# Position attention in a two-layer block: the residual sum moves from VectorE to TensorE and ScalarE

## The reference, cut to what matters

```
hidden = layernorm(x)                                  # [S=8, B=512, H=256]
ln1    = layer_norm(hidden, ln1_weight, ln1_bias)
q,k,v  = split(ln1 @ qkv_weight.T)                     # 16 query heads, 4 key/value heads, 16 wide
attn   = softmax(causal(q . k / 4))                    # over the positions 0..s
ao     = attn . v
h1     = hidden + ao @ proj_weight.T                   # <- the residual sum of this case
ln2    = layer_norm(h1, ln2_weight, ln2_bias)
logits = ln2 @ router_weight                           # then top-2 experts; h1 is also added later
```

## Time and profile before

| | |
|---|---|
| median of 3 runs | 1718.29 us (1713.36 to 1721.59) |
| the profiled execution | 1712.79 us, of which 1711.0 us are the span from its first to its last instruction |
| mean granted TensorE clock | 0.972 of full speed |
| busy shares over the span | PE 93%, DVE 55%, POOL 42%, ACT 37% |

### The profile page before, as it was taken

How to read it: one execution, slowest core, us unless ns; L and a number is a source line. 1 busy time by engine, 2 the same in 40 slices (tenths; PEclk the granted TensorE clock), 3 DMA queues, 4 the chain that set the end, 5 groups by cost and what they waited for, 6 DMA issues and landing times. The chain is left out here.

```text
span 1711.0 us, 33848 instructions
## 1 busy us (share of the span) xinstructions
PE 1596.6 (93%) x11520; PEld 1337.6 (78%) x11520; DVE 934.3 (55%) x2469; ACT 629.0 (37%) x1879; POOL 721.0 (42%) x849
## 2 busy tenths in 40 slices
PE   8999889999999878777699999997999999999998
PEld 6777778887888646676588888885788888888887
DVE  6545536666666695986612222115665565565552
ACT  3333345555555464446411111111333333333331
POOL 3222233333343387973333332315545545445432
PEclk9999989999999999888699999999999999999999
DMA  7686600000000000001433333321000000000000
GB/s 197 128 163 109 111 28 14 14 14 14 13 13 2 17 1 1 25 25 44 141 121 97 110 104 97 99 56 44 29 23 28 21 25 28 18 28 28 19 11 13
DMA packets 92656, 88.58 MB, mean 52 GB/s; under 512 B 11840, under 2 KB 82432, under 8 KB 92160
## 3 DMA queue, kind: packets, MB, share of 16 engines
q1 hardware_dynamic: 73776, 56.63, 13.7%
q0 software_dynamic: 6912, 18.88, 4.2%
q10 hardware_dynamic: 11856, 11.66, 2.0%
HBM read 46.64 MB, written 23.20 MB: 41 GB/s over the span
## 5 line engine op out<-in xcount | busy, mean ns | idle before, releaser
L711 POOL TENSOR_TENSOR probs<-probs,rs 128x384 f32<-128x384 f32 x128 | 105.9, 827 | 212.5 <-DVE rs L886 211.6
L2031 PE MATMUL n_psS<-f_XT,wgu 128*128 128x128 f32 x1536 | 182.2, 275 | 0.9 <-ACT f_XT L2151 0.8
L2031 PEld LDWEIGHTS n_psS<-f_XT,wgu 128*128 128x128 f32 x1536 | 176.6, 192 | 1.7 <-ACT f_XT L2151 1.6
L845 ACT ACTIVATE probs<-psS,nm 128x192 f32<-128x192 f32 x256 | 105.5, 417 | 142.0 <-DVE nm L882 142.0
L1712 POOL DMA_INDIRECT XE<-token_rows,held x80 | 76.1, 951 | 187.7 <-PE e_psX L1731 170.6
L1806 DVE COPY YE<-e_psY 128x512 f32<-128x512 f32 x40 | 27.7, 692 | 224.5 <-PE e_psY L1754 224.5
L1744 PE MATMUL e_psH<-e_XT,w 128*128 128x256 f32 x640 | 145.8, 381 | 0.0
L1754 PE MATMUL e_psY<-w,e_HT 128*128 128x256 f32 x640 | 144.5, 379 | 0.0
L1754 PEld LDWEIGHTS e_psY<-w,e_HT 128*128 128x128 f32 x640 | 121.6, 190 | 16.5
L1782 ACT ACTIVATE e_HT<-e_psH 128x512 f32<-128x512 f32 x80 | 47.7, 597 | 235.9 <-PE e_psH L1744 235.9
L1744 PEld LDWEIGHTS e_psH<-e_XT,w 128*128 128x128 f32 x640 | 119.4, 192 | 14.8
(11 more groups left out here) (277 smaller groups left out, 3435.1 us busy)
## 6 DMA issues: line engine op xcount, KB each, us to landing
KD<-KV SPq DMA_DIRECT2D x256, 66.0 KB, 2.5
expert_out<-YE ACTq DMA_DIRECT2D x40, 256.0 KB, 2.1
w<-in_w SPq DMA_DIRECT2D x16, 512.0 KB, 4.9
X<-in_x SPq DMA_DIRECT2D x8, 512.0 KB, 6.7
x_turned<-XT SPq DMA_DIRECT2D x32, 128.0 KB, 2.3
XS<-x_turned SPq DMA_DIRECT2D x8, 512.0 KB, 4.0
token_rows<-o_XN SPq DMA_DIRECT2D x32, 128.0 KB, 1.7
out_x<-X SPq DMA_DIRECT2D x32, 128.0 KB, 1.7
```

The lines of the kernel that those rows point to most:

```text
L711: nc.gpsimd.tensor_tensor(probs[:, b.q % 4, :, :], probs[:, b.q % 4, :, :], bc(rs[:, b.q % 2, :].unsqueeze(2), [P, 2, KEYS]), ALU.mult).th ...
L845: nc.scalar.activation(probs[:, b.q % 4, u, :], psS[b.q % 2][:, u, :], ACT.Exp, bias=nm[:, b.q % 2, u:u + 1], scale=scale, accum_out=sums[ ...
L2031: mm = pe.matmul(bank[:, m * P:(m + 1) * P], wgu[:, h, f:f + P], FT[:, h, :], start=(m == 0 and h == 0), stop=(m == HALF - 1 and h == KC - ...
```

## The change

Three things change place. (1) TensorE's `project` gets a product with the identity in front: `HS` goes through the identity into the bank, and the two products of the projection accumulate on it. It waits for `h_copied` (row s-2 copied out) and `hs_made` (the input of the sum made) where it waited for `h_added`. (2) ScalarE gets `summed_copied(j, s)`: it waits for `h_ready` and copies the bank over `HS`. It stands in step s+1 behind the copy to `o_AT`. (3) VectorE's `add` loses the addition; bn_stats waits for `h_copied`. Beside these, `folded`, which only turn 4 has, waits for VectorE's own fold of the unit before.

```
@@ TensorE @@
             def project(j, s):
                 pe.wait_ge(a_evac, j * S + s + 1 + 2)
-                pe.wait_ge(h_added, j * S + s + 1)
+                pe.wait_ge(h_copied, j * S + s + 1)
+                pe.wait_ge(hs_made, j * S + s + 1)
+                pe.matmul(psH[s % 2][:, 0:D], k.ident[:, :], k.HS[:, j + s * TS, :], start=True, stop=False)
                 for c in range(KC):
-                    mm = pe.matmul(psH[s % 2][:, 0:D], AT[:, s % 2, c, :], wp[:, c, :], start=(c == 0), stop=(c == KC - 1))
+                    mm = pe.matmul(psH[s % 2][:, 0:D], AT[:, s % 2, c, :], wp[:, c, :], start=False, stop=(c == KC - 1))
                 mm.then_inc(h_ready, 1)
@@ ScalarE @@
+            act.sem_inc(h_copied, 2)
...
+            def summed_copied(j, s):
+
+                act.wait_ge(h_ready, j * S + s + 1 + 2)
+                nc.scalar.copy(k.HS[:, j + s * TS, :], psH[s % 2][:, 0:D]).then_inc(h_copied, 1)
...
                         nc.scalar.copy(AT[:, s % 2, :, :], psA[s % 2][:, :, :]).then_inc(a_evac, 1)
+                    if leaving and 1 <= s <= S:
+                        summed_copied(i - 1, s - 1)
@@ VectorE @@
-            dve.sem_inc(h_added, 2)
...
                 dve.wait_ge(v_made, j * NU + n + 1)
+                if n >= 1:
+                    dve.wait_ge(v_folded, n)
...
             def add(j, s, ch):
-                dve.wait_ge(h_ready, j * S + s + 1 + 2)
+                dve.wait_ge(h_copied, j * S + s + 1 + 2)
                 hs = k.HS[:, bass.ds(j + s * TS, 1), :].rearrange("p a c -> p (a c)")
-                dve.wait_ge(hs_made, j * S + s + 1)
-                ch.step(nc.vector.tensor_tensor(hs, hs, psH[s % 2][:, 0:D], ALU.add))
-                pass_gate(k, dve)
                 nc.vector.bn_stats(k.BST[:, bass.ds(j + s * TS, 1), :].rearrange("p a c -> p (a c)"), hs).then_inc(h_added, 1)
...
-                dve.wait_ge(h_added, j * S + S + 2)
+                dve.wait_ge(h_added, j * S + S)
...
-            ENTER, LEAVE, LAST = S + NO + 2 + 2, S - 4 + 2, 4 + 6 + 1
+            ENTER, LEAVE, LAST = S + NO + 2 + 2, 2, 6 + 1
```

More of the change, by code:

```diff
@@ L994, in position_attention @@
         q_ready, q_copied = k.sem(ctx, "q_ready"), k.sem(ctx, "q_copied")
+        h_copied = k.sem(ctx, "a_h_copied")
         hs_made, v_folded = k.sem(ctx, "a_hs_made"), k.sem(ctx, "a_v_folded")
```

## The result

The changed kernel took 1725.45 us (median of 7 runs, 1722.75 to 1729.83), the kernel before 1718.29 beside it (7 runs). The ratio is 1.0047, with a 95% interval of 1.0029 to 1.0065: 8.0 us slower, 5.0 to 11.2 by the interval (the medians are 7.2 apart). In another series (a2) the changed kernel gave 1.0046 [1.0031, 1.0060]. The forecast was +5.5 us, which the interval holds. The profiled executions took 1722.75 and 1712.8 us, a difference of 9.96. In the series of e1 to e4 one of the 35 runs of the kernel before took 2910 us at a granted clock of 0.735; the ratios leave it out.

The account below looks back on a forecast made before the run. Bound: turn 1's TensorE-ScalarE loop, then VectorE with GpSimd close behind, then TensorE's queue and a TensorE-GpSimd chain. Terms 6.5 - 1.6 - 2.9 + 3.5 = +5.5 us on the median 1718.3 gave 1723.8, say 1724; range 1713 to 1733.

Parts of the forecast that it names:

- Turn 1, +6.5: In turn 1 ScalarE's copy waits for the projection, lengthening five step boundaries by 1.30 us each: +6.5 us.
- VectorE up to turn 2's statistics, -1.6: Up to turn 2's statistics, four additions go (2.3 us) but VectorE waits 0.7 for row 7's copy: -1.6 us.
- Turns 2 and 3, -2.9: In turns 2 and 3 VectorE loses eight additions, but GpSimd becomes the bound and caps the gain: -2.9 us.
- The two waits behind the statistics: Sign of a right forecast: GpSimd's two waits for a buffer VectorE frees shrink from 6.2 to under 2 us.
- Turn 3's end and turn 4, +3.5: From 758.25 us through turn 4, identity products lengthen TensorE's queue and turn 4's start: +3.5 us.
- The two ends of TensorE's queue: At turn 3's end and before the last statistics, three projections each pay 0.43 us for the identity: +1.3 us each.
- turn 4's start: Two projections at low clock stand ahead of the value sums that free GpSimd's unit of 783.17: +0.9 us.
- The first, that the relief goes through: Rival: turn 1 has unseen slack and 24 VectorE additions up to 770 count: -10.2 us, 1708; chance 0.07.
- The second: Rival: TensorE's identity products bound every turn, so turns 2 and 3 gain nothing: +13.1 us, 1731; chance 0.26.
- The third, a faster GpSimd: Rival: fewer additions from turn 2 to turn 4's start speed GpSimd by up to 8.4: -2.9 us, 1715; chance 0.07.

Follow-up runs that it names:

- e1: Kernel before with one more, overwritten product in each projection, the addition staying on VectorE: 1722.68 us, ratio 1.0018.
- e4: Changed kernel with ScalarE's copy of the sum for rows 0 to 4 in turn 1 moved behind the next step's first input tile: 1718.71 us, ratio 0.9995.
- e5: Kernel before with 15 of 32 rows summed by identity and ScalarE, the other 17 added on VectorE: 1718.68 us, ratio 0.9987.
- e6: Changed kernel with the later copy in turn 1 and the identity product issued ahead of its step's value sums: 1725.98 us, ratio 1.0026.
- g0: Kernel before with GpSimd leaving out every fourth product of its units of four from turn 2 on: 1710.91 us, ratio 0.9959.
- g1: Kernel before with GpSimd leaving out every fourth product from turn 2 on and VectorE's additions left out too: 1708.55 us, ratio 0.9938.
- e2: Kernel before with ScalarE in turn 1 also waiting for the projection behind its copy to o_AT, without copy or identity product: 1721.51 us, ratio 1.0018.
- e3: Kernel before with VectorE's additions left out, so the output lacks the residual sum's projection: 1715.92 us, ratio 0.9987.
- e9: Kernel before without additions, GpSimd's fourth score unit in turns 2 and 3 waiting for VectorE's last softmax product: 1715.35 us, ratio 0.9966.
- e7: Kernel before with unused identity products filling TensorE's idle times at the starts of all four turns: 1720.06 us, ratio 0.9991.
- e8: Kernel before with 15 rows summed by identity and ScalarE, plus unused identity products in TensorE's idle times: 1714.91 us, ratio 0.9970.

## Why the prediction was right, and where it was not

*Turn 1, +6.5.* Right in mechanism and size: five boundaries of 1.30 us in both profiled executions; the wait alone gives 0.59 of each, the later copy takes the whole away, and with it the loss. Not forecast were 3.47 and 3.24 us more of low clock in turn 1. They can't simply be counted to the change: e1, e5, e6, g0 and g1, with the boundaries of before, show 2.28, 2.06, 2.72, 0.70 and 2.31 us of it and e2 1.30, while e3, e4 and e9 show none. Nor can they simply be left out: the two amounts of the changed kernel are the largest of all. The mean granted clock over its runs is 0.9686 (7 runs; those beside it have no clock on record) and in a2's series 0.9688 (6 runs) for 0.9696 (12 runs of the kernel before), which can't be told from no difference. If the low clock comes oftener with the longer boundary, it would be part of the 2.5 us by which the measured +8.0 exceeds the forecast; the forecast lies within the interval, and this stays open.

*VectorE up to turn 2's statistics, -1.6.* Measured -1.76. The two bn_stats of rows 6 and 7 take 1.00 us with the wait between them for 0.75 without one, so the wait for the copy is some 0.25 us where I had 0.7. At turn 3 it is 0.40 where I had 0.8.

*Turns 2 and 3, -2.9.* This is the term that was mis-sized: -1.42 and -1.44. That GpSimd would cap the gain was right, and the way there too: it reaches its unit of 746.96 without waiting and sets the pace from there (the unit stands at +7.29, row 6 at +6.21, -1.1 where I had -1.0). But it reaches that unit 10.11 us later than 736.85, where the forecast, with the 2.89 us by which turn 1 came out longer, has 8.69. Three parts make up the 1.42 us. The unit of 704.80 starts 0.27 us later than that sum has it, the two identities and the low clock cost 1.17 us for 0.9, and from 712.06 on GpSimd needs 34.90 us for work that took it 34.02. The last is the largest, 0.88 us, and I had put it at nothing: only 0.18 us of it is a wait, the rest are products that last longer (four take 2.90 us at 712.06 and took 2.36 at 702.83). What lengthens them isn't shown. The two waits behind the statistics shrank from 6.2 to 2.66 us, not under the 2 that I had named. The product held 5.9 us in e3 to e6 isn't held in either profile of the changed kernel (1.52 us), so it doesn't explain this term.

*Turn 3's end and turn 4, +3.5.* The two ends of TensorE's queue are right (+1.36 and +1.35 for 3 x 0.43 each; e1's +3.1 us fits). At turn 4's start I had +0.9. The two profiles have -0.65 and +0.85, and what parts them is TensorE's clock at the value sums of row 1. Timeline of these value sums before, in the changed kernel, and in a2:

```profile
778.65 2.04 PE L1127 MATMUL o_psA<-ident,prodV 128*128 128x128 f32 x8
```

```profile
786.78 1.11 PE L1128 MATMUL o_psA<-ident,prodV 128*128 128x128 f32 x8
```

```profile
787.17 1.92 PE L1128 MATMUL o_psA<-ident,prodV 128*128 128x128 f32 x8
```

The product at low clock is paid for in both (1.01 us where I had 0.86); in the first profile the upper clock is back for the value sums behind it, in a2 as late as before. GpSimd's 13 products start 1.23 us behind the next value sums in the first two of these profiles (781.94 to 783.17, 789.02 to 790.25), so they follow TensorE as forecast. In the first profile two errors, +1.5 and -1.6, cancel, and the terms without the clock of turn 1 sum to 5.4 us for the 5.5 forecast: that agreement is luck. In a2 they sum to 7.0.

*The rivals.* The first, that the relief goes through, is out: no kernel without additions came near -13.7 us, the best of them with a full GpSimd -5.8. The second is out because turns 2 and 3 did gain, 3.2 us, where it had nothing; but its margin was as small as feared. Before row 6 of turn 3 TensorE waited 2.11 us for GpSimd and waits 1.69 in a2; in the first profile the wait lies ahead of row 5 (2.20 us), the low clock behind it fills the time up to row 6, and 0.2 us are left. The third, a faster GpSimd, is out too: its unit of four takes 3.03 and 3.06 us for 3.05 and 3.03 in the earlier trace rows.

## What to carry to other kernels

A wait costs by what is queued behind it: 0.27 us of copying put where the next input tile should have been cost 1.3 us at each boundary and made the change a loss; the same copy one input tile later cost nothing. When the changed kernel runs later, compare the same work and not the same times: a fixed window put 5.3 us of turn 1's waiting into turn 2. Making the second-fullest engine lighter is no clean test of which engine leads: here it also made the fullest engine's own instructions shorter, so read the idle time of both beside it. And when instructions are taken away, look whether one that is left has become slower: e3's held product took 4.5 us more beside a run of GpSimd's, and one wait put that right.

## What was not expected of the hardware

A VectorE product of 128x512 with both inputs in SBUF, issued while GpSimd runs products back to back at the start of turn 2, took either about 1.4 us (with GpSimd's next unit of four at 3.5) or about 5.9 us (with that unit at 2.8; 5.2 beside the lighter GpSimd). The start times don't tell the two apart: in e1 it started 0.69 us behind one GpSimd unit and 0.47 ahead of the next and took 1.42 us, in e3 it started 0.69 behind and 0.47 ahead and took 5.89. It was held in the profiles of e3, e4, e5, e6, g0 and g1 and not in those of the kernel before, e1, e7 and e8. In the changed kernel, a2 and e2 it started 0.1 us behind GpSimd's unit of four and took 1.52 or 1.53 us. What decides it, and how often it happens in executions without a profile, isn't known.

Of the difference from run to run much goes with the clock: over the 35 runs of the kernel before beside e5 to e8, time and mean granted clock have a correlation of -0.80, about 0.9 us per 0.001. Under the fillers the mean is 0.974 (e7) and 0.975 (e8) in place of 0.968; with the mixed rows that kernel was 5 us faster, without them the gain can't be told from none.
